# Keys, queries and values of a batch made in the batch before, over a doubled left-half buffer

## The chip, the cores and the metric

The kernel runs on one core of one Trainium2 chip. The metric is device time in microseconds (us); lower is better. The kernel before takes 324.44 us, the median of three runs (323.96 to 325.45).

## What is computed

The input x is 8 batches of 512 tokens by 256 features. Three residual blocks follow each other, each on a layer norm of its input:

```
x = x + 0.5 * ffn(layernorm(x))      # real(ifft(fft(x) @ w)) + bias
x = x + attn(layernorm(x))           # 16 heads of 8, on the left 128 features alone
x = x + 0.5 * ffn(layernorm(x))      # the same weights again

q = (left @ Wq.T), k = (left @ Wk.T), v = (left @ Wv.T)
att = softmax(q k / 4);  attn = (att v) @ Wo.T + bo
```

## The kernel before, in words

The spectral FFN is folded once into one real 256x256 matrix, half_ffn. What remains for each batch is a pipeline, written out by hand.

**Slots.** The attention of batch `it` is 16 slots (QUADS). In slot s TensorE issues the score matmuls of slot s+1 (`score_quad`, L803), then the jobs of this slot, then the probabilities times values (`value_quad`, L819). In slot 15 the score quad is the first one of batch `it + 1`. ScalarE (ACT) exponentiates two pairs of heads a slot (L665).

**Jobs.** All other matmuls are jobs with names, put into slots by the tables STEADY (batches 1 to 5), BEGIN (0), LATE (6) and END (7), L69 to L90. An entry is (name, which batch relative to `it`, half of the misc bank). F1_t and F2_t are tile t of the first and second FFN (t = 0 to 3; the entry with an "a" is the first of its two accumulation parts), WO_t the output projection, KT_i, QT_i and V_i half i of keys, queries and values, N the norms of q and k for a guard, LT a transpose of the left half. All jobs share one PSUM bank, misc, and a slot's jobs wait until VectorE (DVE) has evacuated all of the slots before (`job`, L721). A half tile of job work is a four-matmul row of 256 columns, 0.45 us; most slots hold two, some one.

**SP's queue.** All transfers of the loop are issued by SP (L496 to L525), in one order and each after its own waits, and an instruction that waits holds all behind it. In a batch they are:

- `k_in`: eight transfers that bring k of batch it+1 from DRAM scratch into the rows of KS (L392);
- `x2_through` and `xT_in_from`: x after attention of batch it-1 is stored (L448) and read back transposed (L454), for F2;
- `load_x`: x and x transposed of batch it+3 (L407, L408);
- `q_out` (L386), then `left_through` (L460), which stores the normalized left half of batch it+2 and waits for DVE's `turn_left`;
- `q_in`, eight transfers into QS (L399), with `leftT_in` (L467) between the fourth and the fifth, which reads the left half back transposed;
- `store_out` of the first half of batch it-1, `k_out` of batch it+2 (L383), `store_out` of the second half.

The first score quad of a batch waits for all its rows of KS and QS (`rows_loaded`, L797). KT_0 and KT_1 of batch it+2 stand in slots 14 and 15 and read leftT; V_0 and V_1 of batch it+1 stand in slots 0 and 1 of the next batch, QT_0 and QT_1 in slots 7 and 8. There is one leftT, so `leftT_in(b)` waits until V and QT of batch b-1 are evacuated. In batch 6 the eight k transfers are split: four, then x2 and xT, then four.

**DVE.** Its order follows the slots (L1209 to L1241). `left_half` and `turn_left` of batch it+2 run at slots 8 and 9, in batch 0 at 7 and 8. `split` (L966) evacuates a half of k or q with a cast and a subtraction.

## Time and profile before

| | |
|---|---|
| median of 3 runs | 324.44 us (323.96 to 325.45) |
| profiled execution | span 327.4 us, on the one core; its own time is not listed apart from the span |
| TensorE (PE) busy | 299.8 us, 92% of the span |
| ScalarE (ACT) busy | 259.0 us, 79% |
| VectorE (DVE) busy | 190.3 us, 58% |
| GpSimd (POOL) busy | 97.8 us, 30% |
| mean granted TensorE clock | 0.995 |
| SP's queue, share of the 16 DMA engines | 53.3% |

Busy time of TensorE is the sum of its matmuls; what is missing to the span is waits and the stretches before the first batch and after the last. The clock is the share of full speed that the chip granted. The chain that ended last is 57% TensorE, 19% transfers and 9% SP's own issuing.

### The profile page before, as it was taken

Reading aid. Unit: us, or ns where it says so; the run is one execution under the profiler, and the core shown is the slowest. Engines: PE = TensorE matmul, PEld = TensorE weight load, DVE = VectorE, ACT = ScalarE, POOL = GpSimd, SP = SyncE. Lnnn points to the kernel's source line nnn. Section 1 sums busy time; section 2 is a strip of 40 time slices with the busy share of each in tenths; the row PEclk is TensorE's granted clock in tenths of the full one; section 3 lists DMA queues with packets and bytes.
Section 4 is the critical chain, followed back from the end, with each engine's and each line's share of the span. In section 5 each row is a group of like instructions: output and inputs, shape, how many; then the busy total and the mean of one; then the engine's idle time right before and its main releaser. Section 6 shows DMA issues by size and latency. Waiting matters only on the chain.

```text
span 327.4 us, 8919 instructions
## 1 busy us (share of the span) xinstructions
PE 299.8 (92%) x3452; PEld 113.8 (35%) x3452; DVE 190.3 (58%) x550; ACT 259.0 (79%) x287; POOL 97.8 (30%) x112
## 2 busy tenths in 40 slices
PE   8598999879998998999997999799997999898995
PEld 5444333233333432343332433233332323222333
DVE  1587438446775676657763677467764743361254
ACT  2114988978897988998995989878997999899921
POOL 6554701212504053033604053223600250034004
PEclk9999999999999999999997999999999999999999
DMA  7834459629654857748652858649354466303002
GB/s 200 298 132 171 104 202 173 175 86 139 209 201 135 188 107 256 225 147 147 237 182 70 188 105 289 193 140 151 114 163 146 102 180 167 109 28 103 35 32 66
DMA packets 29892, 49.87 MB, mean 152 GB/s; under 512 B 3600, under 2 KB 16272, under 8 KB 28944
## 3 DMA queue, kind: packets, MB, share of 16 engines
q1 hardware_dynamic: 29152, 48.79, 53.3%
q8 instruction: 32, 0.52, 0.8%
q10 hardware_dynamic: 688, 0.40, 0.7%
q14 instruction: 20, 0.16, 0.2%
HBM read 31.34 MB, written 17.83 MB: 150 GB/s over the span
## 4 chain that ended last, share of the span: by engine, by line
PE 57%; DMA 19%; SPq 9%; DVE 6%; issue 5%; ACT 3%; POOL 1%; DVEq 0%; ACTq 0%
PE misc L715 21%; PE ot L819 21%; PE scores L803 11%; DMA q_scr<-qp 7%; SPq L399 7%; DMA leftT<-left_scr 5%; DMA QS<-q_scr 4%; ACT probs L665 3%; DMA x_in<-x 2%; PE scores L715 1%; PE misc L689 1%; DVE stats L928 1%; DVE qp L972 1%; PE scores L682 1%; POOL rstd L547 1%
## 5 line engine op out<-in xcount | busy, mean ns | idle before, releaser
L665 ACT ACTIVATE probs<-scores 128x1024 f32<-128x1024 f32 x256 | 244.0, 1030 | 33.2 <-PE scores L803 33.0
L819 PE MATMUL ot<-probs,VS 128*32 128x512 f32 x1024 | 134.9, 598 | 4.8 <-ACT probs L665 3.4
L803 PE MATMUL scores<-QS,KS 32*128 32x512 f32 x512 | 65.0, 497 | 3.2 <-DMA QS<-q_scr 2.2
L803 PEld LDWEIGHTS scores<-QS,KS 32*128 32x128 f32 x512 | 24.6, 182 | 111.3 <-ACT probs L665 100.7
L819 PEld LDWEIGHTS ot<-probs,VS 128*32 128x32 f32 x1024 | 30.9, 110 | 28.4 <-ACT probs L665 7.7
L560 POOL TENSOR_TENSOR x_out<-x,half_bias 128x512 f32<-128x512 f32 x7 | 9.0, 1289 | 102.6 <-DVE x L1001 102.6
L1006 DVE SCALAR_TENSOR_TENSOR x_out<-misc,rstd,x_out 128x256 f32<-128x256 f32 x28 | 13.6, 484 | 38.7 <-PE misc L715 33.8
L545 POOL TENSOR_SCALAR veps<-mv 128x4 f32<-128x4 f32 (+1 forms) x25 | 5.9, 234 | 92.2 <-DVE mv L935 92.2
L715 PE MATMUL misc<-half_ffn,xT 128*32 128x256 f32 x448 | 32.1, 386 | 0.9 <-DMA xT<-x_scr 0.9
L715 PE MATMUL misc<-half_ffn,xT_in 128*32 128x256 f32 x400 | 27.7, 385 | 2.2 <-DVE half_ffn L1177 1.7
L547 POOL TENSOR_TENSOR rstd<-veps,power 128x4 f32<-128x4 f32 (+1 forms) x25 | 25.2, 1008 | 2.1
L928 DVE BATCH_NORM_STATS2 stats<-x 128x6 f32<-128x256 f32 x64 | 23.4, 414 | 0.1
L982 DVE SCALAR_TENSOR_TENSOR x<-misc,rstd,x_in 128x256 f32<-128x256 f32 x24 | 11.6, 484 | 15.6 <-PE misc L715 15.6
L1001 DVE TENSOR_TENSOR x<-misc,x 128x256 f32<-128x256 f32 x30 | 11.4, 420 | 15.3 <-PE misc L715 15.3
L972 DVE CAST kp<-misc 128x256 fp32r<-128x256 f32 x14 | 5.9, 423 | 24.1 <-PE misc L715 24.1
L550 POOL TENSOR_TENSOR x_out<-x,half_bias 128x512 f32<-128x512 f32 x9 | 11.5, 1276 | 19.7 <-DVE x L1001 19.7
L715 PE MATMUL misc<-wo_sb,otn 128*32 128x256 f32 x240 | 16.1, 385 | 0.6 <-DVE otn L1059 0.6
L961 DVE STREAM_TRANSPOSE x_blocks<-x 128x512 f32<-128x512 f32 x14 | 16.2, 1156 | 0.5
L715 PEld LDWEIGHTS misc<-half_ffn,xT 128*32 128x32 f32 x448 | 11.0, 108 | 12.6 <-issue 8.1
L715 PE MATMUL misc<-leftT,wk_sb 128*32 128x256 f32 x112 | 9.0, 405 | 6.4 <-DMA leftT<-left_scr 6.4
L1045 DVE STREAM_TRANSPOSE ot_t<-ot 128x512 f32<-128x512 f32 x16 | 11.4, 716 | 5.2 <-PE ot L819 5.2
L715 PEld LDWEIGHTS misc<-half_ffn,xT_in 128*32 128x32 f32 x400 | 10.3, 109 | 11.7 <-issue 5.6
(126 smaller groups left out, 268.3 us busy)
## 6 DMA issues: line engine op xcount, KB each, us to landing
KS<-k_scr SPq DMA_DIRECT2D x56, 128.0 KB, 4.8
QS<-q_scr SPq DMA_DIRECT2D x56, 128.0 KB, 3.1
x_in<-x SPq DMA_DIRECT2D x8, 512.0 KB, 5.1
xT_in<-x_t SPq DMA_DIRECT2D x8, 512.0 KB, 6.5
k_scr<-kp SPq DMA_DIRECT2D x8, 512.0 KB, 2.7
q_scr<-qp SPq DMA_DIRECT2D x8, 512.0 KB, 4.6
x_scr<-x_blocks SPq DMA_DIRECT2D x7, 512.0 KB, 4.4
xT<-x_scr SPq DMA_DIRECT2D x7, 512.0 KB, 4.5
```

The costliest lines, as they stand in the source:

```text
L399: eng.dma_start(QS[par][first:ROWS * (lane + 1):PARTS, slots, :], q_scr[:, :, heads, :].rearrange("i d h s -> (i d) h s")).then_inc(loaded ...
L547: nc.gpsimd.tensor_tensor(to[:, tiles], veps[k][:, tiles], power[:, tiles], ALU.pow).then_inc(rstd_done[k], 1)
L550: nc.gpsimd.tensor_tensor(dst[:, tiles, :], src[:, tiles, :], row[:, :].unsqueeze(1).to_broadcast([P, tiles.stop - tiles.start, E]), ALU.a ...
L665: nc.scalar.activation(probs[u % PRING][:, :, :], scores[u % SRING][:, :, :], ACT.Exp, scale=SCORE_SCALE).then_inc(exp_done, 1)
L715: last = mm(dst[COL * j:COL * (j + 1), :], weights(j), rhs, start=c == 0, stop=c == len(terms) - 1)
L803: last = mm(scores[(u + j // 2) % SRING][:, j % 2, :], KS[b % 2][rows, slot, kt * P:(kt + 1) * P].bitcast(F32R), QS[b % 2][rows, slot, :]. ...
L819: last = mm(ot[COL * j:COL * (j + 1), :], VS[b % 2][:, kt, h, :], probs[(u + j // 2) % PRING][:, j % 2, :], start=s % 8 == 0, stop=s % 8 == 7)
L928: ins = nc.vector.bn_stats(stats[k][:, t, :], src[:, t, :])
L961: last = nc.vector.transpose(x2_blocks[:, :, 2 * i:2 * i + 2, :], x2[:, 2 * i:2 * i + 2, :].rearrange("p t (f k) -> p k t f", k=E // 32))
L982: return nc.vector.scalar_tensor_tensor(x1[b % 3][:, i, :], tile, rstd[0][b % 2][:, i:i + 1], biased[:, i, :], ALU.mult, ALU.add)
L1001: nc.vector.tensor_tensor(x2[:, i, :], tile, x2[:, i, :], ALU.add).then_inc(evacuated, 1)
L1006: nc.vector.scalar_tensor_tensor(x_out[:, i, :], tile, rstd[2][0][:, i:i + 1], x_out[:, i, :], ALU.mult, ALU.add).then_inc(evacuated, 1)
```

## The change

leftT becomes two buffers, by batch parity, so its load waits for the evacuations of batch b-2. KT of batch it+1 moves to slots 0 and 1 of batch `it`, from slots 14 and 15 of the batch before; V of batch it+1 moves from slots 0 and 1 to slot 9; F2 moves a slot later, to 10 to 15. In BEGIN, QT comes to slot 3, F1 of batch 2 is spread over slots 4 to 8, V over 9 and 10, and KT of batch 2 leaves slot 15. In LATE, KT is in 0 and 1, QT in 5 and 6, V in 7 and 8. On SP `k_out(it + 1)` now stands right before `k_in(it + 1)`, the eight k transfers are no longer split in batch 6, and the second half of an output is stored a batch later. The squares on ACT and, in batch 0, `left_half` and `turn_left` on DVE (slots 10 and 11) move with their inputs.

```diff
--- before.py
+++ after.py
@@ -66,23 +66,22 @@
-STEADY = {0: [("V_0", 1, RIGHT), ("F1_0a", 2, LEFT)], 1: [("F1_0", 2, LEFT), ("V_1", 1, RIGHT)],
+STEADY = {0: [("KT_0", 1, RIGHT), ("F1_0a", 2, LEFT)], 1: [("F1_0", 2, LEFT), ("KT_1", 1, RIGHT)],
           2: [("WO_0", -1, LEFT), ("WO_1", -1, RIGHT)], 3: [("WO_2", -1, LEFT), ("WO_3", -1, RIGHT)],
           4: [("F1_1a", 2, LEFT), ("F1_1", 2, LEFT)], 5: [("F1_2a", 2, LEFT), ("F1_2", 2, LEFT)],
           6: [("F1_3a", 2, LEFT), ("F1_3", 2, LEFT)], 7: [("QT_0", 1, LEFT)], 8: [("QT_1", 1, LEFT)],
-          9: [("F2_0a", -1, LEFT), ("F2_0", -1, LEFT)], 10: [("N", 1, RIGHT), ("F2_1a", -1, LEFT)],
-          11: [("F2_1", -1, LEFT)], 12: [("F2_2a", -1, LEFT), ("F2_2", -1, LEFT)],
-          13: [("F2_3a", -1, LEFT), ("F2_3", -1, LEFT)], 14: [("KT_0", 2, RIGHT)], 15: [("KT_1", 2, RIGHT)]}
-
-BEGIN = {1: [("LT", 1, LEFT)], 2: [("KT_0", 1, LEFT), ("KT_1", 1, RIGHT)],
-         3: [("F1_0a", 2, LEFT), ("F1_0", 2, LEFT)], 4: [("F1_1a", 2, LEFT), ("F1_1", 2, LEFT)],
-         5: [("F1_2a", 2, LEFT), ("F1_2", 2, LEFT)], 6: [("F1_3a", 2, LEFT), ("F1_3", 2, LEFT)],
-         7: [("QT_0", 1, LEFT), ("QT_1", 1, RIGHT)], 8: [("V_0", 1, LEFT), ("V_1", 1, RIGHT)], 10: [("N", 1, RIGHT)],
-         15: [("KT_0", 2, LEFT), ("KT_1", 2, RIGHT)]}
-
-LATE = {0: [("V_0", 1, RIGHT)], 1: [("V_1", 1, RIGHT)],
+          9: [("V_0", 1, RIGHT), ("V_1", 1, LEFT)], 10: [("N", 1, RIGHT), ("F2_0a", -1, LEFT)], 11: [("F2_0", -1, LEFT)],
+          12: [("F2_1a", -1, LEFT), ("F2_1", -1, LEFT)], 13: [("F2_2a", -1, LEFT), ("F2_2", -1, LEFT)],
+          14: [("F2_3a", -1, LEFT)], 15: [("F2_3", -1, LEFT)]}
+
+BEGIN = {1: [("LT", 1, LEFT)], 2: [("KT_0", 1, LEFT), ("KT_1", 1, RIGHT)], 3: [("QT_0", 1, LEFT), ("QT_1", 1, RIGHT)],
+         4: [("F1_0a", 2, LEFT), ("F1_0", 2, LEFT)], 5: [("F1_1a", 2, LEFT)], 6: [("F1_1", 2, LEFT), ("F1_2a", 2, RIGHT)],
+         7: [("F1_2", 2, RIGHT)], 8: [("F1_3a", 2, LEFT), ("F1_3", 2, LEFT)], 9: [("V_0", 1, RIGHT)],
+         10: [("V_1", 1, LEFT), ("N", 1, RIGHT)]}
+
+LATE = {0: [("KT_0", 1, RIGHT)], 1: [("KT_1", 1, RIGHT)],
         2: [("WO_0", -1, LEFT), ("WO_1", -1, RIGHT)], 3: [("WO_2", -1, LEFT), ("WO_3", -1, RIGHT)],
-        6: [("QT_0", 1, LEFT)], 7: [("QT_1", 1, LEFT)],
+        5: [("QT_0", 1, LEFT)], 6: [("QT_1", 1, LEFT)], 7: [("V_0", 1, RIGHT)], 8: [("V_1", 1, LEFT)],
         9: [("F2_0a", -1, LEFT)], 10: [("F2_0", -1, LEFT), ("N", 1, RIGHT)], 11: [("F2_1a", -1, LEFT)], 12: [("F2_1", -1, LEFT)],
         13: [("F2_2a", -1, LEFT)], 14: [("F2_2", -1, LEFT)], 15: [("F2_3a", -1, LEFT), ("F2_3", -1, LEFT)]}
 END = {2: [("WO_0", -1, LEFT), ("WO_1", -1, RIGHT)], 3: [("WO_2", -1, LEFT), ("WO_3", -1, RIGHT)],
@@ -239,7 +238,7 @@
         rstd = [[sb(f"rstd{i}_{j}", [P, T]) for j in range(2 if i == 0 else 1)] for i in range(3)]
 
         xT = sb("xT", [P, C, P // 32, T, 32])
-        leftT = sb("leftT", [P, S])
+        leftT = [sb(f"leftT{i}", [P, S]) for i in range(2)]
         left_blocks = sb("left_blocks", [P, HD // 32, T, 32])
         x2_blocks = sb("x2_blocks", [P, E // 32, T, 32])
 
@@ -461,10 +460,12 @@
                              left_blocks[:, :, :, :].rearrange("p k t s -> p (k t s)")).then_inc(left_stored, 16)
 
             def leftT_in(b):
-                for kind in ("V", "QT"):
-                    sp.wait_ge(evacuated, last_count(kind, b - 1))
+                for kind in ("KT", "QT") if b == 2 else ("KT", "QT", "V"):
+                    sp.wait_ge(evacuated, last_count(kind, b - 2))
+                if b == 2:
+                    sp.wait_ge(first_v_ready, 1)
                 sp.wait_ge(left_stored, 16 * (b - 1))
-                sp.dma_start(leftT[:, :].rearrange("p (g s) -> p g s", g=P // 32),
+                sp.dma_start(leftT[b % 2][:, :].rearrange("p (g s) -> p g s", g=P // 32),
                              left_scr.rearrange("g f k s -> (f k) g s")).then_inc(left_loaded, 16)
 
             def store_out(b, i):
@@ -496,15 +497,14 @@
             for it in range(B):
                 if it == 0:
                     load_x(3)
-                    k_out(1)
+                if it >= 2:
+                    store_out(it - 2, 1)
                 if it + 1 < B:
-
-                    k_in(it + 1, range(0, LANES // 2 if it == B - 2 else LANES))
+                    k_out(it + 1)
+                    k_in(it + 1, range(LANES))
                 if it >= 1:
                     x2_through(it - 1)
                     xT_in_from(it - 1)
-                if it == B - 2:
-                    k_in(it + 1, range(LANES // 2, LANES))
                 if it >= 1 and it + 3 < B:
                     load_x(it + 3)
                 if it + 1 < B:
@@ -519,10 +519,7 @@
                     q_in(it + 1, range(2, LANES))
                 if it >= 1:
                     store_out(it - 1, 0)
-                if it + 2 < B:
-                    k_out(it + 2)
-                if it >= 1:
-                    store_out(it - 1, 1)
+            store_out(B - 2, 1)
             store_last_out(B - 1)
             sp.wait_ge(out_stored, 32 * (B - 1) + 16 * T)
 
@@ -656,9 +653,9 @@
                 it, s = divmod(u, PAIRS)
                 if it + 1 < B:
 
-                    if s == (2 * 2 if it else 2 * 5):
+                    if s == (2 * 4 if it else 2 * 5):
                         square(kp, sq_k, kp_step, it + 1)
-                    if s == (2 * 10 if it else 2 * 9):
+                    if s == (2 * (8 if it == B - 2 else 10) if it else 2 * 7):
                         square(qp, sq_q, qp_step, it + 1)
                 act.wait_ge(scores_ready, u // 2 + 1)
                 wait(act, quad_done, (u - PRING) // 2 + 1)
...
@@ -1226,9 +1223,9 @@
                                 norm_stats(2, x2, t, t == T - 1)
                             norm_moments(2, it)
                     if it + 2 < B:
-                        if s == (8 if it else 7):
+                        if s == (8 if it else 10):
                             left_half(it + 2, range(0, 2))
-                        if s == (9 if it else 8):
+                        if s == (9 if it else 11):
                             left_half(it + 2, range(2, T))
                             turn_left(it + 2)
                     if it + 3 < B:
```

**TensorE, end of batch 1 and begin of batch 2.** leftT,wk_sb is KT, wv_sb,leftT V, half_ffn,xT F2, half_ffn,xT_in F1; QS,KS is a score quad, probs,VS a value quad. Before, from slot 14 of batch 1 to slot 1 of batch 2:

```order
L715 MATMUL misc<-leftT,wk_sb 32x256 x4
L819 MATMUL ot<-probs,VS 32x512 x4
L803 MATMUL scores<-QS,KS 128x512 x4
L715 MATMUL misc<-leftT,wk_sb 32x256 x4
L819 MATMUL ot<-probs,VS 32x512 x4
L803 MATMUL scores<-QS,KS 128x512 x4
L715 MATMUL misc<-wv_sb,leftT 32x128 x8
L715 MATMUL misc<-half_ffn,xT_in 32x256 x4
L819 MATMUL ot<-probs,VS 32x512 x4
L803 MATMUL scores<-QS,KS 128x512 x4
L715 MATMUL misc<-half_ffn,xT_in 32x256 x4
L715 MATMUL misc<-wv_sb,leftT 32x128 x8
```

And now:

```order
L712 MATMUL misc<-half_ffn,xT 32x256 x4
L816 MATMUL ot<-probs,VS 32x512 x4
L800 MATMUL scores<-QS,KS 128x512 x4
L712 MATMUL misc<-half_ffn,xT 32x256 x4
L816 MATMUL ot<-probs,VS 32x512 x4
L800 MATMUL scores<-QS,KS 128x512 x4
L712 MATMUL misc<-leftT,wk_sb 32x256 x4
L712 MATMUL misc<-half_ffn,xT_in 32x256 x4
L816 MATMUL ot<-probs,VS 32x512 x4
L800 MATMUL scores<-QS,KS 128x512 x4
L712 MATMUL misc<-half_ffn,xT_in 32x256 x4
L712 MATMUL misc<-leftT,wk_sb 32x256 x4
```

KT has left the last two slots for the first two, where it takes the place of V, and F2 fills the slots that it left.

**SP, batch 6.** KS<-k_scr are the k rows, x_scr<-x_blocks the store of x2, xT<-x_scr its way back. Before:

```order
L383 DMA k_scr<-kp 128x1024
L472 DMA out<-x_out 128x512
L392 DMA KS<-k_scr 16x4x512 x4
L448 DMA x_scr<-x_blocks 128x1024
L454 DMA xT<-x_scr 128x8x128
L392 DMA KS<-k_scr 16x4x512 x4
L386 DMA q_scr<-qp 128x2x512
```

And now:

```order
L382 DMA k_scr<-kp 128x1024
L391 DMA KS<-k_scr 16x4x512 x8
L447 DMA x_scr<-x_blocks 128x1024
L453 DMA xT<-x_scr 128x8x128
L385 DMA q_scr<-qp 128x2x512
```

All eight k transfers stand ahead of x2, and the k store ahead of them belongs to the same batch. In batches 1 to 5 the order on SP is the old one, but for an output store that has gone ahead of the k store.

**DVE, batch 0.** lh and left_blocks are the left half of batch 2, norms to safe the job N, VS the evacuation of V. Before:

```order
L1045 STREAM_TRANSPOSE ot_t<-ot 128x512
L946 TENSOR_SCALAR lh<-x_2,mv,rstd_0 128x128 x2
L1019 COPY VS<-misc 128x16x8 x4
L946 TENSOR_SCALAR lh<-x_2,mv,rstd_0 128x128 x2
L955 STREAM_TRANSPOSE left_blocks<-lh 128x512
L1027 TENSOR_REDUCE norms<-misc 128x1
L1029 STREAM_TRANSPOSE norm_row<-norms 128x32
L1033 TENSOR_TENSOR norm_max<-norm_row 1x16 x2
L1035 TENSOR_TENSOR norm_prod<-norm_max 1x16
L1037 TENSOR_REDUCE worst<-norm_prod 1x1
L1039 TENSOR_SCALAR safe<-worst 1x1
```

And now:

```order
L932 BN_AGGR mv<-stats 128x2 x4
L1016 COPY VS<-misc 128x16x8 x4
L1024 TENSOR_REDUCE norms<-misc 128x1
L1026 STREAM_TRANSPOSE norm_row<-norms 128x32
L1030 TENSOR_TENSOR norm_max<-norm_row 1x16 x2
L1032 TENSOR_TENSOR norm_prod<-norm_max 1x16
L1034 TENSOR_REDUCE worst<-norm_prod 1x1
L1036 TENSOR_SCALAR safe<-worst 1x1
L943 TENSOR_SCALAR lh<-x_2,mv,rstd_0 128x128 x4
L952 STREAM_TRANSPOSE left_blocks<-lh 128x512
```

The left half was ahead of N and is behind it.

## Rows read from the trace of the kernel before

**Rows 1.** TensorE timeline: first score quads of batches 1 to 7.
```profile
67.50 0.51 PE L803 MATMUL scores<-QS,KS 32*128 32x512 f32 x4 [1.20 <-DMA QS<-q_scr]
...
103.92 0.51 PE L803 MATMUL scores<-QS,KS 32*128 32x512 f32 x4
...
139.59 0.51 PE L803 MATMUL scores<-QS,KS 32*128 32x512 f32 x4 [0.35 <-DMA QS<-q_scr]
...
177.25 0.80 PE L803 MATMUL scores<-QS,KS 32*128 32x512 f32 x4
...
213.60 0.51 PE L803 MATMUL scores<-QS,KS 32*128 32x512 f32 x4
...
249.60 0.51 PE L803 MATMUL scores<-QS,KS 32*128 32x512 f32 x4
...
281.54 0.51 PE L803 MATMUL scores<-QS,KS 32*128 32x512 f32 x4 [0.62 <-DMA QS<-q_scr]
```

**Rows 2.** Table of waits, TensorE.
```profile
PE misc L715 <- DMA leftT<-left_scr: 6.4, 4, 2.0
```

**Rows 3.** Stretches: length, PE, PEld, DVE, ACT, POOL, PEclk, DMA, GB/s.
```profile
172.00:177.50 5.50, 3.45 (x28) 1.16 (x24) 1.67 (x8) 2.12 (x3) 3.72 (x4) 0.73 0.32 101
```

**Rows 4.** TensorE in order of time, batches 2 and 6.
```profile
105.79 0.51 PE L803 MATMUL scores<-QS,KS 32*128 32x512 f32 x4
...
108.09 0.51 PE L803 MATMUL scores<-QS,KS 32*128 32x512 f32 x4
...
127.04 1.07 PE L715 MATMUL misc<-half_ffn,xT 128*32 128x256 f32 x16 [0.92 <-DMA xT<-x_scr]
...
269.64 0.64 PE L715 MATMUL misc<-half_ffn,xT 128*32 128x256 f32 x8
```

**Rows 5.** SP's queue in order of time, batch 2.
```profile
105.97 0.33 SPq L383 DMA_DIRECT2D k_scr<-kp  x1
...
108.71 3.61 SPq L392 DMA_DIRECT2D KS<-k_scr  x8
116.24 0.34 SPq L448 DMA_DIRECT2D x_scr<-x_blocks  x1
121.16 0.66 SPq L454 DMA_DIRECT2D xT<-x_scr  x1
...
125.77 0.38 SPq L386 DMA_DIRECT2D q_scr<-qp  x1
...
130.75 2.40 SPq L399 DMA_DIRECT2D QS<-q_scr  x4
```

**Rows 6.** DMA, 104 to 140 us, 40 slices: busy tenths, GB/s.
```profile
DMA  0008935999999998400024999995007964796570
GB/s 9 18 0 360 385 130 175 187 116 127 125 130 125 130 164 291 164 23 9 0 53 123 332 409 398 387 405 225 30 5 284 253 182 163 229 336 191 121 287 20
```

**Rows 7.** SP's queue in order of time, batches 1 and 6.
```profile
73.50 3.60 SPq L392 DMA_DIRECT2D KS<-k_scr  x8
...
84.39 0.69 SPq L454 DMA_DIRECT2D xT<-x_scr  x1
...
261.29 0.34 SPq L448 DMA_DIRECT2D x_scr<-x_blocks  x1
263.98 0.65 SPq L454 DMA_DIRECT2D xT<-x_scr  x1
```

**Rows 8.** DVE in order of time, batch 2.
```profile
105.52 0.42 DVE L974 TENSOR_TENSOR kp<-misc,kp 128x256 fp32r<-128x256 f32 x1
...
109.67 0.48 DVE L982 SCALAR_TENSOR_TENSOR x<-misc,rstd,x_in 128x256 f32<-128x256 f32 x1 [0.35 <-PE misc L715]
```

**Rows 9.** SP's queue, batch 0: the left half of batch 2.
```profile
57.26 0.34 SPq L460 DMA_DIRECT2D left_scr<-left_blocks  x1
```

**Rows 10.** DVE in order of time, batch 0.
```profile
56.07 1.17 DVE L955 STREAM_TRANSPOSE left_blocks<-lh 128x512 f32<-128x512 f32 x1
...
59.26 0.14 DVE L1039 TENSOR_SCALAR safe<-worst 1x1 int32<-1x1 f32 x1
```

More of the change, by code:

```diff
@@ L756, in job @@
                     if b == 0:
-                        last = by_columns(bank[:, :], [(columns_of(weights), leftT[:, :])])
+                        last = by_columns(bank[:, :], [(columns_of(weights), leftT[b % 2][:, :])])
                     else:
-                        last = by_columns(half, [(columns_of(weights), leftT[:, i * E:(i + 1) * E])])
+                        last = by_columns(half, [(columns_of(weights), leftT[b % 2][:, i * E:(i + 1) * E])])
                 elif kind == "V_":
                     for t in range(2):
-                        last = by_columns(half[:, t * HD:(t + 1) * HD], [(columns_of(leftT, (2 * i + t) * P), wv_sb[:, :])])
+                        last = by_columns(half[:, t * HD:(t + 1) * HD], [(columns_of(leftT[b % 2], (2 * i + t) * P), wv_sb[:, :])])
                 elif name == "N":
@@ L776, in first_v @@
                 for t in range(T):
-                    last = by_columns(first_v_bank[:, t * HD:(t + 1) * HD], [(columns_of(leftT, t * P), wv_sb[:, :])])
+                    last = by_columns(first_v_bank[:, t * HD:(t + 1) * HD], [(columns_of(leftT[0], t * P), wv_sb[:, :])])
                 last.then_inc(first_v_ready, 1)
@@ L1008, in evacuate @@
                 elif name == "LT":
-                    nc.vector.tensor_copy(leftT[:, :].rearrange("p (g t s) -> p t g s", g=P // 32, t=T),
+                    nc.vector.tensor_copy(leftT[b % 2][:, :].rearrange("p (g t s) -> p t g s", g=P // 32, t=T),
                                           bank.rearrange("p (t g s) -> p t g s", g=P // 32, t=T)).then_inc(evacuated, 1)
```

## The prediction

> **What bounds the kernel now.** I call T0 of a batch the moment its first score quad starts; it stands in slot 15 of the batch before. The seven T0s [rows 1] are 36.42, 35.67, 37.66, 36.35, 36.00 and 31.94 us apart (batches 1 to 6). TensorE is nearly always busy, so first I ask what a batch costs without waits. From T0 to slot 0 is 1.87 us (105.79 - 103.92), a slot with half a tile of job work; slot 0 itself, with two halves, takes 2.30 (108.09 - 105.79) [rows 1, 4]. The steady table has ten slots of the second kind, five of the first and one with N that I put at 2.1: 34.4 us is TensorE's own length, and 1 to 3 us of each batch are waits.
>
> The table of waits gives TensorE 6.4 us in four waits on the load of leftT, the longest 2.0 us [rows 2]. They are the waits this change aims at: KT of batch it+2 in slots 14 and 15, right behind the load. Behind the longest, the stretch from 172.0 to 177.5 shows a granted clock of 0.73, part of it at 1.2 GHz [rows 3]. Batch 3, less its wait and TensorE's own length, leaves 37.66 - 2.0 - 34.4, about 1.2 us, as the cost of that.
>
> The second thing to see is that the leftT wait hides another. The q rows decide T0 too: three of the seven T0s show a wait on them (1.20, 0.35, 0.62) [rows 1]. Follow SP's queue in batch 2, T0 = 103.92 [rows 5]: k stored at +2.05, k rows from +4.79, x2 stored at +12.32, xT asked for at +17.24, q stored at +21.85, q rows from +26.83, and the next T0 at +35.67, held by them. The transfers form a ladder, and it is already longer than TensorE's 34.4. With leftT earlier and all else equal, batch 2 would gain nothing and the others little.
>
> **The change part by part.**
>
> *Job work, 0.* Every tile job is still done. In the steady table KT takes the place of V in slots 0 and 1, V's two halves fill slot 9, and F2 goes a slot later; slots 14 and 15 keep half a tile each. In batch 6 two more halves go in slots where ACT sets the pace. Batch 0 loses the KT of slot 15 and spreads F1_1, F1_2 and V thinner: three slots fall from 2.30 to 1.87, one rises by 0.2, about 1 us less on TensorE. I count it as 0, since T0 of batch 1 is set by transfers (below). Both squares move with their inputs and stay on ACT: 0.
>
> *The four leftT waits, -6.4 and their clock -1.2.* Gone: the load lands in batch it-1 and is read 2 us after T0. The sum below replaces whole batches, so this gain is inside it.
>
> *k leaves later.* KT_1 is in slot 1. DVE begins that slot's evacuations at T0 + 5.75 (109.67), with F1_0 for 0.48, then the cast and the subtraction of kp, 0.42 each [rows 8]: k is stored from +7.05, 5.0 us later than now. k rows start 2.74 us after it [rows 5]: +9.8. SP issues the eight for 3.6 us, so x2, ready at +12.3 as before, is issued at +13.4. That 1.1 us is the small part.
>
> *x2 stands behind the k rows.* While k rows move, the DMA engines are full (nines at about 130 GB/s from 108.7 to 117), and only after that comes the burst of x2's store [rows 6]. Issued near their end it is through 4.92 us later; in batch 6, where only half of the k rows precede it and they are through, it takes 2.69 [rows 5, 7]. From the first k row to the next rung I read 12.45 (batch 2) and 10.89 (batch 1) [rows 5, 7]. I take 11.5, between them, as the store's own tail can no longer be its late issue; the ends stay for the range. The Trainium skill, "DMA: Bandwidth & Descriptors", section on queues, rings and completion order, says that each engine takes descriptors in ring order, which agrees, but also that completion is not first in, first out, which speaks against my price; by it the store could be through 4.92 us after its issue, and the whole sum would be 331 (second rival).
>
> *xT and q.* xT is then asked for at 7.05 + 2.74 + 11.5 = +21.3 instead of +17.2. It is used 5.9 us after the request (127.04 - 121.16), at +27.2; F2_0a, a slot later than F2_0 is now, would want it at +24.5 (22.2 + 2.3) [rows 4, 5]: a new wait of about 2.7 us replaces the present 0.92. The x loads follow, and q's store behind them. From xT's request to q's rows is 9.59 us with both x loads (130.75 - 121.16), and from there to T0 8.84 [rows 5]. Sum of the ladder: 7.05 + 2.74 + 11.5 + 9.59 + 8.84 = 39.7 us. TensorE with its new wait would be ready at 37 and stands behind it, so batches 1 to 4 take 39.7 each, 158.8 for 146.1 now [rows 1]: **+12.7**. Batch 5 loads no x: 1 MB less at 400 GB/s [rows 6] is 2.6 us, so 37.1 for 36.0: **+1.1**.
>
> *Batch 6.* Its k rows are not split any more. With half tiles in slots 0 and 1, k leaves near +6.2, k rows +8.9, xT asked for +20.4, here 5 us later (at most 5.7 in rows 4 and 7; no x loads): +25.4. Its F2_0a stays in slot 9, at +20.0 now [rows 1, 4]. So 5.4 us of wait, less the 0.62 at the end: **+4.8**.
>
> *Batch 0.* F1_3 of batch 2 goes from slot 6 to 8 and the left half from slots 7 and 8 to 10 and 11, on DVE now behind N. N ended at 59.40 and still does within 0.3; then the transpose of 1.17 and before it the four lh, which I estimate at as much again, give 61.8 [rows 10]. SP sends left_scr there and holds the q rows of batch 1 behind it. It was sent at 57.26, and T0 of batch 1 came 10.2 us later [rows 1, 9]: **+4.4**, a wait above 5 us on an idle TensorE.
>
> *Clock.* A wait of 2.0 us cost 1.2 us once [rows 2, 3]; the three others, 1.5 us on average, left batches 1, 4 and 5 no such rest. I charge it behind the two long waits (batch 1's T0, batch 6's FFN): **+2.4**. Between lie the others; charging none or all is in the range.
>
> *More waits, 0.* V's evacuation in slot 9 delays DVE's left half by some 0.5 us, and its store waits behind q's anyway. The last out half of a batch goes a batch later; GpSimd wants that tile some 11 us after T0.
>
> Sum: 12.7 + 1.1 + 4.8 + 4.4 + 2.4 = +25.4. The profiled span of 327.4 would become 352.8; it is 3.0 above the median of the plain runs, 324.44, and I carry the same difference: **350 us**. A measurement tells about 0.5% (1.6 us).
>
> **The rivals.**
>
> *x2 passes the k rows.* Its store takes 4.92 from its issue at +13.4, so xT is asked for at +18.4, and the ladder is 36.8. Batches 2 to 4 come to 110.5, batch 1 to 38.1 with its clock, batch 5 to 34.4, batch 6 to 33.3, and T0 of batch 7 to 288 instead of 281.5: **331**. Against it: the order of the bursts in rows 6. 0.12.
>
> *Every wait costs the clock.* If the waits before T0, about 2 us each, all bring 1.2 GHz, KT_1 in slot 1 is late too and each of four more batches pays 1.2; with 12.45 in place of 11.5 five times: **355 to 360**. 0.16.
>
> *The other side, faster.* The ladder is only long because TensorE let it be, and KT in slot 1 costs it nothing. It decides at one point: the q rows must be in within 34.4 us of T0, so xT asked for by T0 + 16. Then 6.4 + 1.2 + 1.2 of waits go: **316**. Against it: x2 alone is issued at +13.4, and 2.69 is the best a store took. 0.06.
>
> *The change does not bite*, gains and delays cancel: **324**. 0.04.
>
> **How the numbers follow.** My case, 0.62, spans 346 to 355 by the tail of x2's store (10.9 to 12.45, in five batches). The range takes in the clock's rival and nearly x2's: 330 to 361. Slower 0.62 + 0.12 + 0.16 = 0.90, same 0.04, faster 0.06.
>
> **What would show it.** T0s 39 to 41 us apart in batches 1 to 4, T0 of batch 1 near 72; no wait on leftT; xT as a wait of 2 to 3 us in front of F2_0a and of 5 in batch 6; k rows issued near T0 + 10 and x2's store done near T0 + 21; more time at 1.2 GHz. If x2 is through by T0 + 18.5, or left_scr goes out before 59 in batch 0, I am wrong.

## The result and the profile after

| | before | after |
|---|---|---|
| median | 324.94 us (323.96 to 328.48, 4 runs) | 359.88 us (357.46 to 362.33, 4 runs) |
| ratio after to before | | 1.109, 95% interval 1.104 to 1.115 |
| profiled execution: span | 327.4 us | 360.5 us |
| TensorE busy | 299.8 us, 92% | 312.7 us, 87% |
| mean granted TensorE clock | 0.995 | 0.957 |
| SP's queue, share of the 16 DMA engines | 53.3% | 49.1% |

The change costs 35 us. It moves the same bytes and computes the same matmuls; TensorE's 13 us more of busy time are matmuls at a lower clock, and the rest are waits. Medians, here and below, are over all executions of a kernel, while a ratio and its interval leave out the slow ones and compare with the kernel before as measured beside that run (medians 323.15 to 324.94).

A profile shows one execution, and not the median one. Wherever both are on record, the time is the span plus 1.75 to 1.95 us. The profiled execution of the changed kernel is thus the longest of its four (362.33 us), and that of the kernel before, whose own time is not on record, would be about 329 us, some 4 us above its median.

The table of waits, TensorE, of the changed kernel (us in total, times, longest) answers to [rows 2]:

```profile
PE scores L800 <- DMA QS<-q_scr: 24.5, 6, 5.4
PE misc L712 <- DMA xT<-x_scr: 8.5, 6, 4.4
```

There is no row for leftT any more. The waits on the q rows have grown from 2.2 us to 24.5 and those on xT from 0.9 to 8.5. The TensorE timeline shows where; these are the first score quads of batches 1 to 7, as [rows 1]:

```profile
70.05 0.80 PE L800 MATMUL scores<-QS,KS 32*128 32x512 f32 x4 [5.41 <-DMA QS<-q_scr]
...
111.98 0.51 PE L800 MATMUL scores<-QS,KS 32*128 32x512 f32 x4 [4.64 <-DMA QS<-q_scr]
...
152.77 0.51 PE L800 MATMUL scores<-QS,KS 32*128 32x512 f32 x4 [3.36 <-DMA QS<-q_scr]
...
194.34 0.80 PE L800 MATMUL scores<-QS,KS 32*128 32x512 f32 x4 [4.80 <-DMA QS<-q_scr]
...
235.79 0.80 PE L800 MATMUL scores<-QS,KS 32*128 32x512 f32 x4 [4.40 <-DMA QS<-q_scr]
...
276.19 0.51 PE L800 MATMUL scores<-QS,KS 32*128 32x512 f32 x4 [1.86 <-DMA QS<-q_scr]
...
314.69 0.51 PE L800 MATMUL scores<-QS,KS 32*128 32x512 f32 x4
```

T0 of batch 7 is 33.15 us later than before, as much as the whole span has grown (33.1), so nothing behind it matters. Batch by batch, T0 to T0:

| batch | before | after | more | forecast, clock apart |
|---|---|---|---|---|
| 1 | 36.42 | 41.93 | 5.51 | 3.3 |
| 2 | 35.67 | 40.79 | 5.12 | 4.0 |
| 3 | 37.66 | 41.57 | 3.91 | 2.0 |
| 4 | 36.35 | 41.45 | 5.10 | 3.4 |
| 5 | 36.00 | 40.40 | 4.40 | 1.1 |
| 6 | 31.94 | 38.50 | 6.56 | 4.8 |

With batch 0, whose T0(1) is 2.55 us later, this is the 33.15. SP's queue in order of time shows one batch of it, batch 2 with T0 = 111.98, to be laid beside [rows 5]:

```profile
120.60 0.33 SPq L382 DMA_DIRECT2D k_scr<-kp  x1
123.33 3.61 SPq L391 DMA_DIRECT2D KS<-k_scr  x8
127.03 0.37 SPq L447 DMA_DIRECT2D x_scr<-x_blocks  x1
134.46 0.66 SPq L453 DMA_DIRECT2D xT<-x_scr  x1
135.17 0.67 SPq L406 DMA_DIRECT2D x_in<-x  x1
135.89 1.27 SPq L407 DMA_DIRECT2D xT_in<-x_t  x1
137.20 0.43 SPq L385 DMA_DIRECT2D q_scr<-qp  x1
139.56 0.33 SPq L459 DMA_DIRECT2D left_scr<-left_blocks  x1
143.59 3.39 SPq L398 DMA_DIRECT2D QS<-q_scr  x4
```

k is stored at +8.62, where it was +2.05. The store of x2 now takes 7.43 us (127.03 to 134.46) instead of 4.92. Behind the x loads q's store needs 6.39 us until its rows are asked for, and these start at +31.61 instead of +26.83. The stretches show the third part, the clock, behind the T0s of batches 2 and 5, then behind the T0 of batch 6, and last in batch 6 behind the wait on xT (columns as in [rows 3], the last but two the granted clock):

```profile
112.00:117.50 5.50, 5.50 (x48) 1.73 (x48) 1.66 (x4) 3.45 (x4) 0.00 (x0) 0.69 0.13 49
235.00:242.00 7.00, 6.21 (x44) 2.17 (x48) 1.23 (x3) 3.85 (x4) 0.00 (x0) 0.52 0.15 56
276.00:281.50 5.50, 5.31 (x60) 1.75 (x60) 3.40 (x8) 4.74 (x6) 0.00 (x0) 1.00 0.14 51
300.00:307.00 7.00, 5.94 (x40) 1.73 (x40) 1.09 (x4) 1.94 (x2) 0.00 (x0) 0.51 0.61 179
```

After each of the five waits of 3.4 to 5.4 us on q rows TensorE runs at 1.2 GHz for a part of the next slots (the mean granted clock of these stretches is 0.52 to 0.72), and so it does behind the 4.4 us on xT in batch 6; after the 1.86 us at 276.19 it does not.

Last, the table of waits of SP. Of the kernel before:

```profile
SPq L448 <- DVE x_blocks L961: 31.5, 7, 9.2
SPq L453 <- DMA x_scr<-x_blocks: 22.2, 6, 4.6
SPq L460 <- DVE left_blocks L955: 20.4, 6, 4.1
SPq L386 <- DVE qp L974: 17.7, 7, 4.1
```

And of the changed one:

```profile
SPq L452 <- DMA x_scr<-x_blocks: 36.0, 6, 7.0
SPq L398 <- DMA q_scr<-qp: 23.7, 6, 5.0
SPq L459 <- DVE left_blocks L952: 22.8, 6, 10.1
SPq L447 <- DVE x_blocks L958: 9.2, 1, 9.2
SPq L385 <- DVE qp L971: 0.8, 2, 0.5
```

The wait of q's store on DVE has all but gone (17.7 us before, 0.8 now): q is ready before SP comes to it. In its place SP waits for q's store to land, 23.7 us. The store of x2 has changed sides in the same way: before, SP waited seven times for DVE to have x2 ready, now only once, and otherwise comes late itself. That difference explains two experiments below.

### The profile page after: what moved, and what is told of

It reads as the page before. It is cut to its first block, busy times and chain, and to the rows that moved or that the text cites. A ratio compares the mean times of both kernels' runs of the same rounds, so it can differ in the third digit from the quotient of the medians.

```text
span 360.5 us, 8924 instructions
## 1 busy us (share of the span) xinstructions
PE 312.7 (87%) x3452; PEld 117.0 (32%) x3452; DVE 189.9 (53%) x550; ACT 259.8 (72%) x287; POOL 97.5 (27%) x112
## 3 DMA queue, kind: packets, MB, share of 16 engines
q1 hardware_dynamic: 29152, 48.79, 49.1%
## 4 chain that ended last, share of the span: by engine, by line
PE 45%; DMA 27%; SPq 12%; DVE 8%; issue 5%; ACT 2%; POOL 1%; DVEq 0%; ACTq 0%
PE misc L712 16%; PE ot L816 15%; PE scores L800 8%; DMA x_scr<-x_blocks 8%; DMA q_scr<-qp 6%; SPq L398 6%; DMA QS<-q_scr 6%; DMA xT<-x_scr 4%; SPq L391 4%; DMA k_scr<-kp 3%; ACT probs L662 2%; PE scores L679 2%; PE scores L712 1%; PE scores L686 1%; DVE kp L971 1%
## 5 line engine op out<-in xcount | busy, mean ns | idle before, releaser
L816 PE MATMUL ot<-probs,VS 128*32 128x512 f32 x1024 | 140.2, 620 | 3.6 <-ACT probs L662 2.6
L800 PE MATMUL scores<-QS,KS 32*128 32x512 f32 x512 | 67.1, 513 | 25.2 <-DMA QS<-q_scr 24.5
L712 PE MATMUL misc<-half_ffn,xT 128*32 128x256 f32 x448 | 35.8, 413 | 8.5 <-DMA xT<-x_scr 8.5
L816 PEld LDWEIGHTS ot<-probs,VS 128*32 128x32 f32 x1024 | 32.0, 113 | 29.0 <-ACT probs L662 6.2
L712 PE MATMUL misc<-half_ffn,xT_in 128*32 128x256 f32 x400 | 28.6, 394 | 1.8 <-DVE half_ffn L1174 1.3
L544 POOL TENSOR_TENSOR rstd<-veps,power 128x4 f32<-128x4 f32 (+1 forms) x25 | 25.2, 1008 | 2.1
L1042 DVE STREAM_TRANSPOSE ot_t<-ot 128x512 f32<-128x512 f32 x16 | 11.5, 717 | 18.9 <-PE ot L816 18.8
L998 DVE TENSOR_TENSOR x<-misc,x 128x256 f32<-128x256 f32 x30 | 11.4, 420 | 13.5 <-PE misc L712 13.5
L712 PEld LDWEIGHTS misc<-half_ffn,xT 128*32 128x32 f32 x448 | 10.5, 111 | 22.0 <-issue 19.3
L547 POOL TENSOR_TENSOR x_out<-x,half_bias 128x512 f32<-128x512 f32 x9 | 11.5, 1278 | 19.7 <-DVE x L998 19.7
L925 DVE BATCH_NORM_STATS2 stats<-x_in 128x6 f32<-128x256 f32 x32 | 11.8, 412 | 2.8 <-issue 2.8
```

The source lines that it names most:

```text
L544: nc.gpsimd.tensor_tensor(to[:, tiles], veps[k][:, tiles], power[:, tiles], ALU.pow).then_inc(rstd_done[k], 1)
L547: nc.gpsimd.tensor_tensor(dst[:, tiles, :], src[:, tiles, :], row[:, :].unsqueeze(1).to_broadcast([P, tiles.stop - tiles.start, E]), ALU.a ...
L712: last = mm(dst[COL * j:COL * (j + 1), :], weights(j), rhs, start=c == 0, stop=c == len(terms) - 1)
L800: last = mm(scores[(u + j // 2) % SRING][:, j % 2, :], KS[b % 2][rows, slot, kt * P:(kt + 1) * P].bitcast(F32R), QS[b % 2][rows, slot, :]. ...
L816: last = mm(ot[COL * j:COL * (j + 1), :], VS[b % 2][:, kt, h, :], probs[(u + j // 2) % PRING][:, j % 2, :], start=s % 8 == 0, stop=s % 8 == 7)
L925: ins = nc.vector.bn_stats(stats[k][:, t, :], src[:, t, :])
```

## The experiments

The edits are short diffs against the changed kernel first, then against the one before. Periods are T0 to T0 of the profiled execution; the profiled executions of x_behind_q, split_in_6, three_mended and left_own_queue are 3 to 8 us above the median of their kernel, so from them single waits are read, and the sums come from the medians. The ratios carry 0.3 to 0.8% either way. A gain of about 4 us on the changed kernel is 1.2 to 1.4% between two of them: clear of the noise, but its size is known to 2 or 3 us only.

**The store of x2 on a queue of its own** (x2_own_queue).

```diff
                 if it >= 1:
-                    x2_through(it - 1)
                     xT_in_from(it - 1)
...
                 pool.wait_ge(evacuated, evac_count(f"WO_{T - 1}", b))
+                pool.wait_ge(x2_turned, b + 1)
+                wait(pool, xT_loaded, 16 * b)
+                pool.dma_start(x2_scr.rearrange("g f k s -> (g f) (k s)"),
+                               x2_blocks[:, :, :, :].rearrange("p k t s -> p (k t s)")).then_inc(x2_stored, 16)
```

> The changed kernel with one thing different: GpSimd issues the store of x2 on its own queue, right after the WO evacuations, instead of SP behind the k rows. Theory (the store is late because it stands behind eight k transfers in one queue; it was done 7.4 us after its issue): on a queue of its own it is done within 3 to 5 us, xT is asked for by T0 + 19 instead of T0 + 22.5, the burst of xT follows the k rows without a gap, and each T0 of batches 2 to 5 comes some 2 us earlier: 349 to 352 us. Rival (the 16 engines are simply full, the queue does not matter): the store still takes about 7 us, T0s stay 41 us apart, 358 to 361 us.

Measured 356.17 us (353.65 to 357.35), ratio to the kernel before 1.098 (1.092 to 1.104): 3.7 us less than the changed kernel, less than half of what the theory wanted (349 to 352), and more than the rival gave (358 to 361). The detail of its line, the seven stores on GpSimd's queue:

```profile
DMA to landing us min/median/max: 3.6/6.9/7.6
```

On SP's queue the median was 7.0. A queue of its own does not get the store past the k rows. What each queue moved tells why. The store of batch 6 is issued at 280.47; these are packets, MB and share of the 16 engines, first from 281 to 284 us and then from 285 to 287:

```profile
q1 hardware_dynamic: 245, 0.40, 106.4%
```

```profile
q0 software_dynamic: 132, 0.50, 82.4%
q1 hardware_dynamic: 24, 0.02, 7.9%
```

q1 is SP's queue with the k rows, q0 GpSimd's with the store; a share near 100% or above is all 16 engines taken. While the k rows fill the engines, not a packet of the store moves, and it follows when they are through. The store at 317.74, with no k rows in flight, moves most of its packets between 319 and 320 and lands after 3.6 us. The Trainium skill, "DMA: Bandwidth & Descriptors", section "Queues, rings and completion order", says that an engine takes turns between its queues packet by packet; a store would then have moved among the k rows from the start. This trace does not agree. Whether the engines held it back or its packets came to them late, no run here shows.

In batch 2 the store left no earlier than in the changed kernel, at +15.28 against +15.05: DVE's second transpose into x_blocks ends at +14.75 there. So in steady batches x2's store is held by two things at once, SP busy with the k rows (to +14.96 in the changed kernel, forecast +13.4) and DVE, which has x2 ready late (+14.05), since slots 15 and 0 run partly at 1.2 GHz.

**The x loads behind q's store** (x_behind_q).

```diff
-                if it >= 1 and it + 3 < B:
-                    load_x(it + 3)
                 if it + 1 < B:
                     q_out(it + 1)
+                if it >= 1 and it + 3 < B:
+                    load_x(it + 3)
```

> The changed kernel with load_x(it + 3) issued after q_out instead of before it. Theory (q's store stands behind the two x loads, 1 MB at 400 GB/s): from the request of xT to the q rows 7 instead of 9.1 to 10.1 us, as in batch 5 now (7.4), T0s of batches 2 to 5 each 2 to 2.6 us earlier, 350 to 352 us. Rival (q's store takes 5 to 6 us whatever stands before it): no change, 358 to 361 us. Third: DVE waits for x in slot 11 and gives part of it back.

Measured 345.69 us (344.27 to 354.01), ratio 1.064 (1.058 to 1.069): 14 us less than the changed kernel, more than expected (350 to 352), and the largest single piece. Its waits on q rows fall from 24.5 us to

```profile
PE scores L800 <- DMA QS<-q_scr: 18.5, 6, 5.5
```

and SP's queue in batch 2 (T0 = 110.54) shows how q leaves earlier:

```profile
131.59 0.66 SPq L453 DMA_DIRECT2D xT<-x_scr  x1
132.54 0.42 SPq L385 DMA_DIRECT2D q_scr<-qp  x1
133.02 1.47 SPq L406 DMA_DIRECT2D x_in<-x  x1
...
138.35 2.40 SPq L398 DMA_DIRECT2D QS<-q_scr  x4
...
145.70 0.38 SPq L468 DMA_DIRECT2D leftT<-left_scr  x1
```

From xT's request to the q rows are 6.76 us instead of 9.13, and over the four batches with x loads this rung is 11.2 us shorter. But a part comes back in the next rung: the x loads now run beside the left half's store, SP waits for it to land before it asks for leftT (145.70), and the last q rows stand behind that. In batch 2 the rung from the q rows to T0 grows from 9.18 to 12.95 us, and the batch takes 40.76 us, as long as before. The clock gives something too: the four shorter executions were granted 0.970 to 0.980 on average, the changed kernel's four 0.953 to 0.957. How the 14 us divide between these the one profile, of an execution 8 us above the median, doesn't show.

**TensorE kept busy before it waits** (awake). Sixteen bf16 matmuls, 3.63 us at 2.4 GHz, are added ahead of each wait for the rows; they are work that the changed kernel doesn't do.

```diff
-                elif b and s == 0:
-                    pe.wait_ge(rows_loaded, ROW_SIGNALS * b)
                 u = PAIRS * b + 2 * s
                 wait(pe, exp_done, u + 2 - SRING)
+                if b and s == 0:
+                    keep_awake(16, scores[u % SRING][:, 0, :])
+                    pe.wait_ge(rows_loaded, ROW_SIGNALS * b)
```

> The changed kernel with 16 bf16 matmuls (3.5 us at full clock) on zeros in front of the wait for a batch's rows, into a score bank that is free, batches 1 to 7; they add work, no result uses them. Clock theory (five T0 waits of 1.9 to 5.4 us each put the first slots at 1.2 GHz, and k leaves at T0 + 8.6 instead of + 7.4): no stretch at 1.2 GHz behind a T0, k stored at T0 + 7.4, 353 to 355 us. Rival (the slow stretch runs beside transfers and costs nothing, or the added matmuls cost as much as they save): 358 to 362 us.

Measured 355.72 us (353.70 to 358.21), ratio 1.097 (1.088 to 1.105), just above the 353 to 355 of the theory and below the rival's 358. The stretch behind T0 of batch 2, and the one of batch 6 with the wait for xT:

```profile
110.00:117.50 7.50, 7.40 (x98) 2.87 (x97) 4.64 (x10) 6.69 (x8) 0.00 (x0) 1.00 0.12 43
...
286.00:294.00 8.00, 3.90 (x28) 1.17 (x28) 0.00 (x0) 2.36 (x4) 0.00 (x0) 0.66 0.51 164
```

The clock stays at 2.4 GHz behind every T0. k is stored at +6.8 to +7.0 in batches 1 to 5, which is the +7.05 of the prediction; so the 1.6 us of k's lateness are the clock's. Batches 1 to 5 take 39.20, 38.50, 40.19, 39.19 and 38.32, together 10.7 us less than in the changed kernel. Of that only 4.2 us arrive in the median. Batch 6 takes 41.34 instead of 38.50, since at its end the rows are in already and the added matmuls stand there for nothing:

```profile
303.53 3.63 PE L686 MATMUL scores<-waking 128*128 128x512 bf16 x16
```

The two profiled spans differ by 7.6, and they come from a long execution of the changed kernel and a short one of this kernel, so the 10.7 is at the upper end of what the clock costs there. An estimate from the medians is the 4.2 us and the 2.8 that batch 6 gives back: about 7.

**Batch 0: the q rows ahead of the left half** (q_rows_first).

```diff
                     q_out(it + 1)
+                if it == 0:
+                    q_in(it + 1, range(LANES))
                 if it + 2 < B:
                     left_through(it + 2)
-                if it + 1 < B:
+                if it and it + 1 < B:
                     q_in(it + 1, range(0, 2))
...
-                if it + 1 < B:
+                if it and it + 1 < B:
                     q_in(it + 1, range(2, LANES))
```

> The changed kernel, in batch 0 alone with all eight q transfers of batch 1 before left_through and leftT_in of batch 2. Theory (the 5.4 us wait at T0 of batch 1 is the left half on DVE behind N, with the q rows held behind it in SP's order): q rows are issued from about 55 us, T0 of batch 1 comes near 65.0 instead of 70.05 with full clock, and leftT, now late, costs at most 1.5 us at KT_0: 353 to 356 us. Rival (the q rows are late by the DMA engines, not by order): T0 of batch 1 stays above 68, 358 to 361 us.

Measured 354.09 us (348.62 to 356.49, four runs; none reaches the changed kernel's lowest, 357.46). T0 of batch 1 comes at 63.67 instead of 70.05, without a wait, so the left half on SP's queue did hold it. Batch 1 then takes 42.59, with 1.75 us of wait on leftT before its first KT: 0.7 of the 6.4 go back at once. By the medians the order of these transfers in batch 0 costs 5.8 us; with four executions spread over 7.9 us no ratio was formed, and the size is rough.

**k's rows split again in batch 6** (split_in_6).

```diff
-                    k_in(it + 1, range(LANES))
+                    k_in(it + 1, range(0, LANES // 2 if it == B - 2 else LANES))
                 if it >= 1:
                     x2_through(it - 1)
                     xT_in_from(it - 1)
+                if it == B - 2:
+                    k_in(it + 1, range(LANES // 2, LANES))
```

> The changed kernel with one part undone: in batch 6 the eight k transfers are split as before, four, then x2 and xT, then four. Theory (the 4.4 us wait for xT in batch 6 and the 1.2 GHz behind it come from x2's store standing behind all eight): wait under 1.5 us at full clock, batch 6 takes 35 to 36 us instead of 38.5, now by the q rows: 356 to 358 us against 360. Rival (k leaves so late that the split does not help): batch 6 stays above 38.

Measured 355.53 us (351.25 to 358.71), ratio 1.096 (1.087 to 1.104): 4.4 us less. xT is asked for at +15.5 instead of +19.7, the wait on it falls from 4.39 to 0.51, no 1.2 GHz follows, and batch 6 takes 33.15 instead of 38.50 (expected 35 to 36). At the next T0 a wait of 1.24 us on the q rows shows that was hidden.

**The three that helped, together** (three_mended): the edits of x_behind_q, q_rows_first and split_in_6 in one kernel.

> The changed kernel with three of the single edits together: x loads behind q_out, the q rows of batch 1 ahead of the left half of batch 2, and the k transfers split in batch 6. Theory (the parts of the loss are separate terms on one chain: 360 less some 13, 4 to 6 and 4 to 5 us): 336 to 340 us, T0s of batches 2 to 5 still 38 to 40 us apart, because k still leaves in slot 1 with x2, xT and q behind it. Rival (the waits replace one another): above 345 us. Other rival (with these mended the change itself gains): below 324 us.

Measured 332.54 us (330.65 to 338.79), ratio 1.022 (1.015 to 1.029), below what was expected (336 to 340). Alone the three gave 14.2, 5.8 and 4.4, which sums to 24.4; in one kernel they give 27.3. The granted clock fits that: it is 0.995 to 1.000 in the four shorter executions, so nearly all of the lower clock has gone with the waits. The changed order of jobs can thus be had for 8 us more than the kernel before, not 35. Its waits on the q rows, in a profiled execution 6 us above the median:

```profile
PE scores L804 <- DMA QS<-q_scr: 10.9, 6, 3.0
```

In the queue k is still stored at +7.0 to +9.8 in batches 1 to 5, and xT still asked for at +20.4 to +23.0.

**On the kernel before: the second leftT alone** (left_double). Two buffers by parity and the release from batch b-2, as in the change; the jobs stay where they were.

```diff
-        leftT = sb("leftT", [P, S])
+        leftT = [sb(f"leftT{i}", [P, S]) for i in range(2)]
...
-                for kind in ("V", "QT"):
-                    sp.wait_ge(evacuated, last_count(kind, b - 1))
+                for kind in ("KT", "QT") if b == 2 else ("KT", "QT", "V"):
+                    sp.wait_ge(evacuated, last_count(kind, b - 2))
+                if b == 2:
+                    sp.wait_ge(first_v_ready, 1)
```

> The kernel before, with the second buffer for leftT alone and its load waiting for batch b-2; tables and SP's order as before. Theory (the load is late because it is issued late, after q's store; the single buffer never held it): no wait goes, 323 to 326 us. Rival (the buffer held the load): the four leftT waits shrink, 316 to 320 us.

Measured 323.54 us (322.06 to 328.13, ten runs), ratio 1.002 (0.999 to 1.005): no difference in time. The waits on leftT are 1.4 us in its profile, where the kernel before has 6.4:

```profile
PE misc L717 <- DMA leftT<-left_scr: 1.4, 2, 0.8
```

That is not the buffer's doing. SP's waits in the kernel before have no row in which leftT's load waits for V or QT to be evacuated, so the single buffer did not hold it. And x_first below, with one buffer, shows as little:

```profile
PE misc L715 <- DMA leftT<-left_scr: 1.6, 2, 1.1
```

The profile before is of an execution some 4 us above the median, so a part of its 6.4 us is likely that execution's own, though no second profile of that kernel shows it.

**On the kernel before: KT_0 beside KT_1 in slot 15** (kt_in_15), which gives leftT a slot more to arrive.

```diff
-          13: [("F2_3a", -1, LEFT), ("F2_3", -1, LEFT)], 14: [("KT_0", 2, RIGHT)], 15: [("KT_1", 2, RIGHT)]}
+          13: [("F2_3a", -1, LEFT), ("F2_3", -1, LEFT)], 15: [("KT_0", 2, LEFT), ("KT_1", 2, RIGHT)]}
```

> The kernel before, with KT_0 moved from slot 14 to slot 15, beside KT_1, in batches 1 to 5; nothing else. The load of leftT has 2 us more, so its waits (6.4 us in all) and the slow clock behind one of them should be gone. Theory (leftT's wait hides the q rows, which hold T0 at + 35.7 to 36.4 by themselves): T0s stay 35.6 to 36.5 us apart, TensorE shows a wait on the q rows of 1.3 to 2 us at every one of them, and the time moves by no more than 2 us: 322 to 326 us. Rival (leftT was the bound): T0s 34.4 to 34.8 us apart, 315 to 318 us.

Measured 329.82 us (326.26 to 336.55), ratio 1.014 (1.008 to 1.021): a miss, 322 to 326 us were expected. The leftT waits are gone, and at all seven T0s stands

```profile
PE scores L803 <- DMA QS<-q_scr: 9.6, 7, 2.3
```

That is 7.4 us more on the q rows for the 6.4 saved on leftT, as if the leftT wait had hidden them. But the move makes a part of these waits itself: in batch 2 k is stored at +3.3 instead of +2.0, xT asked for at +17.7 instead of +17.2 and q stored at +22.9 instead of +21.9. The run does not separate the two. It does show that a later k and q go with a loss, of 1.4%.

**On the kernel before: the x loads at the batch's start** (x_first).

```diff
+                if it >= 1 and it + 3 < B:
+                    load_x(it + 3)
                 if it + 1 < B:
...
-                if it >= 1 and it + 3 < B:
-                    load_x(it + 3)
```

> The kernel before, with load_x(it + 3) issued at the start of a batch, before the k rows, instead of between xT and q. Theory (the q ladder holds T0 of the kernel before too, and the two x loads are a part of it): q stored by T0 + 26.2 instead of 26.8, T0s 0.5 us closer in batches 1 to 4, leftT lands that much earlier too: 320 to 323 us. Rival (no share of them, or the k rows lose what q gains, as they now stand behind the x loads): 324 to 327 us.

Measured 325.15 us (322.78 to 326.21, ten runs), ratio 1.004 (1.001 to 1.008): nothing gained. The k rows now stand behind the loads, and xT is asked for at +17.5 to +19.3, not earlier; q is stored at +21.9, as before, in batches 2 to 4.

**On the kernel before: the left half on GpSimd's queue** (left_own_queue). `left_through` and `leftT_in` leave SP for a function of GpSimd, called behind its norm of each batch, and SP issues the eight q rows in one piece.

```diff
-                if it + 2 < B:
-                    left_through(it + 2)
                 if it + 1 < B:
-                    q_in(it + 1, range(0, 2))
-                if it + 2 < B:
-                    leftT_in(it + 2)
-                if it + 1 < B:
-                    q_in(it + 1, range(2, LANES))
+                    q_in(it + 1, range(LANES))
...
+                    left_round(it + 2)
```

> The kernel before, with the two transfers of the left half issued by GpSimd on its own queue, and SP's eight q transfers in one piece; tables as before. Theory (the kernel before is held at T0 by the q rows and, tied with them, by leftT; SP issues both in one order): the q rows land about 1 us earlier after T0 and leftT 1 to 2 us earlier, T0s 34.5 to 35.3 us apart: 318 to 321.5 us. Rival (the transfers share the engines, so the order does not matter): 322 to 325 us.

Measured 332.54 us (331.19 to 337.81), ratio 1.024 (1.018 to 1.030): a miss, the theory wanted 318 to 321.5. The q rows hold no T0 behind batch 1's, but leftT does:

```profile
PE misc L709 <- DMA leftT<-left_scr: 11.2, 5, 3.0
```

Its transfers, KB each and us to landing (median), against 2.0 and 5.0 on SP's queue in the kernel before:

```profile
left_scr<-left_blocks POOLq DMA_DIRECT2D x6, 256.0 KB, 3.2
leftT<-left_scr POOLq DMA_DIRECT2D x6, 256.0 KB, 5.4
```

Both take longer here, and they now run beside the q rows. The queue alone need not be the reason: in old_x_behind_q the same store on SP's queue has a median of 3.1. Four of these waits, of 2.2 to 3.0 us, have a stretch at 1.2 GHz behind them, the fifth, of 1.3 us, has none.

**The same with the x loads behind q's store** (left_own_x_behind): the edits of left_own_queue and of x_behind_q together, on the kernel before.

> As left_own_queue, and load_x(it + 3) issued after q_out. Theory: q's store no longer stands behind the x loads (it was issued 4.6 us after xT here, so there is less to gain than in the changed kernel): 0 to 1.5 us below left_own_queue. Rival (the x loads now stand before the q rows, or DVE waits for x in slot 11): up to 2 us above it.

Measured 334.06 us (332.21 to 339.73), ratio 1.027 (1.020 to 1.034): no better than left_own_queue, where 0 to 1.5 us less were expected. In batches 2 to 4 the q rows go out at +25.1 to +25.2, 1.2 to 2.1 us earlier than before, and TensorE waits for leftT for 11.4 us instead.

**On the kernel before: the x loads behind q's store** (old_x_behind_q), the edit of x_behind_q on the other kernel.

> The kernel before with one edit: load_x(it + 3) issued after q_out instead of before it, in batches 1 to 4. Theory (x loads stand in front of q's store; with the left half on GpSimd's queue this edit brought q's store from T0 + 26 to 27 down to T0 + 25.2): q rows are issued from T0 + 25.6, held then by the left half's own turn, leftT is asked for 1 us earlier, T0s 34.5 to 35.5 us apart in batches 2 to 5: 319 to 322.5 us, the first version below the kernel before. Rival (what q gains the x loads take from leftT and the q rows behind them): 323.5 to 326 us.

Measured 326.08 us (323.88 to 332.51, twelve runs), ratio 1.010 (1.006 to 1.014): a small loss, where 319 to 322.5 were expected and where the same edit gave the changed kernel 14 us. SP's waits in this kernel:

```profile
SPq L386 <- DVE qp L974: 25.5, 7, 4.8
SPq L460 <- DVE left_blocks L955: 14.9, 6, 3.4
```

Here q's store waits for DVE, to +21.9 with or without the x loads ahead of it, and the q rows stand behind the left half's store, which waits for DVE to about +25.5. The loads fitted into the time before q was ready, and moved behind it they run beside q's rows. In the changed kernel q is ready before SP reaches it, so whatever stands ahead of its store is on the path.

No version tried is faster than the kernel before.

## Why the prediction was right, and where its numbers were off

**Slower, near 350.** The direction, the mechanism and the places came as forecast: no wait on leftT, waits on q rows at T0, xT in front of F2, T0 of batch 1 late. The time is 359.88, 10 us above the number and 1 us inside the range; two of the four executions lie above 361. My main case, 346 to 355 at 0.62, did not come, and the range held because it was stretched for a rival. 7.7 of the 10 us are in the sum (forecast +25.4, spans +33.1). The other 2.4 come from the step to the median: the span before stood 3.0 above it and I carried that over, but the changed kernel's stands only 0.6 above its own (360.5 against 359.88).

**k leaves later, forecast +7.05, measured +8.6 to +8.8, +9.9 in batch 5.** This rung was mis-sized by the clock. DVE's evacuations of slot 1 begin at T0 + 7.3 in batch 2 (119.30), not at T0 + 5.75, because slots 15 and 0 run partly at 1.2 GHz. In awake they begin at T0 + 5.73, and k is back at +6.8 to +7.0. The first row of these evacuations in the changed kernel, and then in awake, where T0 is 109.54:

```profile
119.30 0.48 DVE L979 SCALAR_TENSOR_TENSOR x<-misc,rstd,x_in 128x256 f32<-128x256 f32 x1
```

```profile
115.27 0.48 DVE L980 SCALAR_TENSOR_TENSOR x<-misc,rstd,x_in 128x256 f32<-128x256 f32 x1
```

I had charged the clock behind two waits only and added its 1.2 us outside the ladder; where a wait stands in front of T0, its clock delays the next batch's k, and so the next T0 and the next wait. It feeds itself.

**x2 behind the k rows, forecast 11.5 from the first k row to xT's request, measured 11.1** in batch 2 and 10.8 to 11.2 in the others. Right. The first rival, that x2 passes the k rows, is dead (the prediction once calls it the second), and x2_own_queue says that not even another queue lets it pass.

**From xT's request to the q rows, forecast 9.59, measured 9.1 to 10.1, and 7.4 in batch 5** (forecast 7.0). Right in size, not in what it was made of. In the kernel before this rung held two waits for DVE, of q's store for qp and of left_scr for the left half; now it is the x loads and q's store landing behind them. I had read the ladder before as transfers alone. In the middle SP stood 17.7 us in seven waits for qp, time in which the x loads cost nothing, and neither x_first nor old_x_behind_q could gain by moving them.

**The last rung, forecast 8.84, measured 9.1 to 9.5.** Right. With these rungs batch 2 is 8.62 + 2.73 + 11.13 + 9.13 + 9.18 = 40.8, as measured; I had 39.7, and 39.7 for batches 1, 3 and 4 that took 41.5 to 41.9.

**The wait for xT in steady batches, forecast 2.7, measured 0.5 to 1.15.** TensorE reaches F2_0a later than I said (+26.5 in batch 2, forecast +24.5), since its slots were slower by the clock. It was off the path, as argued.

**Batch 6, forecast +4.8 and 1.2 of clock, measured +6.6.** xT was asked for at +19.7 (forecast +20.4) and waited for 4.4 us (5.4):

```profile
301.06 1.08 PE L712 MATMUL misc<-half_ffn,xT 128*32 128x256 f32 x8 [4.39 <-DMA xT<-x_scr]
```

split_in_6 confirms that the undivided k rows are the cause.

**Batch 0, forecast +4.4, measured +2.55** at T0 of batch 1. The left half went out at 60.91, I had 61.8:

```profile
60.91 0.34 SPq L459 DMA_DIRECT2D left_scr<-left_blocks  x1
```

and T0 came 9.1 us behind, not 10.2. Its 5.41 us of wait were as said, and q_rows_first shows that queue order made them.

**The clock, forecast +2.4 in all.** This is the term that failed. It was charged twice; the profile shows it six times, behind the waits at the T0s of batches 1 to 5 and in batch 6, and through k it sits in the ladder as well. awake puts it at 7 (an estimate from the medians) to 10.7 us (the profiles) over batches 1 to 5, which is 1.4 to 2.1 for each. The second rival, every wait costs the clock at 355 to 360, had 0.16 and was the case that came: its price of 1.2 us for each wait was too low and its x2 term (12.45, measured 11.1) too high, so that its number fits partly by luck.

**The leftT waits.** They were forecast as gone without gain, because the q rows stood behind them. Gone they are, and the second buffer alone changed no time (left_double). That the q rows would have taken their place is less sure. Where the leftT waits were small by themselves, the q-row waits were little larger than the 2.2 us before: 2.8 in left_double and 3.3 in x_first, with batches 2 to 5 taking 34.6 to 35.5 us instead of 35.7 to 37.7. kt_in_15 speaks for it, but with a later q. The prediction read one long execution of the kernel before as its usual course.

What stays open: the remaining 8 us of three_mended were not taken apart by a run. That they are k's late start is argued from its queue and from kt_in_15's direction, not shown. The 14 us of x_behind_q are taken apart only in part.
